# A two-layer mixture-of-experts kernel: plain result rows per token, tiles in three levels of completeness, and a scatter in eight that waits for the one ahead of it

## What is computed

```
x = x + attn_a(layernorm(x))   # grouped causal attention, 8 kv heads x 4, rotary
x = x + ffn(layernorm(x))      # called "f" in the kernel
x = x + attn_b(layernorm(x))   # causal difference attention, 16 heads
x = x + ffn(layernorm(x))      # called "h" in the kernel, same weights

def ffn(x):                    # T = 2048 tokens, 16 experts of width 176
    scores = softmax(x @ Wg.T)                      # (T, 16)
    keep the 2 best of 4 groups of experts, then the 4 best experts (topi)
    combine = 0 everywhere but scores at topi
    h = silu(x @ W1[e]) * (x @ W3[e])               # for each expert e
    y = sum over e of (h @ W2[e]) * combine[:, e]
    z = silu(x @ Ws1.T) * (x @ Ws3.T) @ Ws2.T       # shared expert, width 352
    return y + z
```

## Time and profile before

| | |
|---|---|
| time, median of 3 runs | 1354.8 us (1343.55 to 1356.92) |
| the profiled execution's own time | 1349.85 us |
| its span, first to last instruction | 1348.1 us |
| mean granted TensorE clock | 0.934 of full speed |
| busy: TensorE, VectorE, GpSimd, ScalarE | 1144.7, 873.5, 689.1, 541.6 us |
| DMA | 169.84 MB, mean 126 GB/s |

### The profile page before, as it was taken

How to read it: one execution, slowest core, us unless ns; L and a number is a source line. 1 busy time by engine, 2 the same in 40 slices (tenths; PEclk the granted TensorE clock), 3 DMA queues, 4 the chain that set the end, 5 groups by cost and what they waited for, 6 DMA issues and landing times.

```text
span 1348.1 us, 26055 instructions
## 1 busy us (share of the span) xinstructions
PE 1144.7 (85%) x8706; PEld 614.0 (46%) x8706; DVE 873.5 (65%) x2067; ACT 541.6 (40%) x846; POOL 689.1 (51%) x841
## 2 busy tenths in 40 slices
PE   6888999998899699999288899999779859999990
PEld 2343444342655366566154344444246435665650
DVE  5688899981576145555388899999568523554543
ACT  2124777779431122222032577777844001222210
POOL 4452344544036577767552454545521652787671
PEclk9897999999889799999699899999988978999995
DMA  4424433320825479987754321221062345898868
GB/s 144 144 86 126 122 109 121 106 64 2 287 72 149 150 183 164 158 156 113 192 178 143 108 61 53 62 50 50 3 255 48 113 129 144 168 159 161 153 91 262
DMA packets 145875, 169.84 MB, mean 126 GB/s; under 512 B 20240, under 2 KB 130768, under 8 KB 145232
## 3 DMA queue, kind: packets, MB, share of 16 engines
q1 hardware_dynamic: 115856, 128.79, 32.7%
q0 software_dynamic: 29184, 38.36, 16.7%
q10 hardware_dynamic: 704, 1.02, 0.2%
HBM read 93.29 MB, written 76.18 MB: 126 GB/s over the span
## 4 chain that ended last, share of the span: by engine, by line
PE 57%; DVE 18%; issue 6%; DMA 6%; ACT 6%; POOL 2%; SPq 2%; another core or an unknown queue 1%; POOLq 0%; ACTq 0%; DVEq 0%
PE pair_ps L1996 11%; PE o_ps L1761 9%; ACT arena L849 4%; DVE nm L1123 4%; PE pair_ps L2029 4%; DMA x_slots<-y_sb,slot_i 3%; DVE bm L1123 3%; PE pair_ps L2032 2%; PE t_ps L1787 2%; PE pair_ps L1711 2%; PE pair_ps L1592 2%; PE pair_ps L1691 2%; PE pair_ps L1716 2%; PE pair_ps L2003 2%; PE pair_ps L1686 2%
## 5 line engine op out<-in xcount | busy, mean ns | idle before, releaser
L849 ACT ACTIVATE arena<-pair_ps 128x1024 f32<-128x1024 f32 x320 | 322.9, 1024 | 130.6 <-PE pair_ps L1686 75.9
L625 POOL TENSOR_SCALAR_AFFINE_SELECT arena<-arena 128x512 f32<-128x512 f32 (+1 forms) x320 | 175.0, 547 | 241.4 <-ACT arena L849 240.9
L1123 DVE TENSOR_REDUCE nm<-pair_ps 128x2 f32<-128x1024 f32 (+1 forms) x192 | 232.6, 1222 | 33.4 <-PE pair_ps L1735 29.5
L687 POOL DMA_INDIRECT x_slots<-y_sb,slot_i x128 | 123.6, 966 | 168.0 <-DVE slot_i L1321 94.0
L1761 PE MATMUL o_ps<-arena 128*9 128x512 f32 (+7 forms) x2048 | 176.8, 440 | 4.2 <-POOL arena L625 4.1
L1996 PE MATMUL pair_ps<-arena 128*128 x512 | 168.6, 471 | 2.5 <-ACT arena L900 2.5
L1123 DVE TENSOR_REDUCE bm<-pair_ps 128x8 f32<-128x1024 f32 x128 | 155.3, 1217 | 4.1 <-PE pair_ps L1735 1.0
L703 POOL DMA_INDIRECT y_h<-xnT,dest x80 | 125.3, 1567 | 58.6 <-DVE xnT L1480 31.4
L703 POOL DMA_INDIRECT y_f<-xnT,dest x80 | 124.6, 1558 | 42.0 <-issue 21.2
L1463 DVE TENSOR_TENSOR arena<-arena,pair_ps 128x128 f32<-128x128 f32 x144 | 41.4, 288 | 116.6 <-ACT arena L905 77.1
L1996 PEld LDWEIGHTS pair_ps<-arena 128*128 128x128 f32 x512 | 93.8, 195 | 43.9 <-issue 6.3
(11 more groups left out here) (275 smaller groups left out, 2012.8 us busy)
## 6 DMA issues: line engine op xcount, KB each, us to landing
arena<-x_slots SPq DMA_DIRECT2D x128, 132.5 KB
arena<-in_w SPq DMA_DIRECT2D x4, 2816.0 KB, 18.9
arena<-q_a SPq DMA_DIRECT2D x64, 96.0 KB
arena<-q_b SPq DMA_DIRECT2D x64, 96.0 KB
y_f<-hw SPq DMA_DIRECT2D x11, 512.0 KB, 2.9
y_h<-hw SPq DMA_DIRECT2D x11, 512.0 KB, 2.9
arena<-in_w SPq DMA_DIRECT2D x2, 2048.0 KB, 17.4
arena<-y_f SPq DMA_DIRECT2D x8, 512.0 KB
```

Source lines behind the costliest of these rows:

```text
L625: pool.affine_select(p, p, pattern, ALU.is_ge, 0.0, base=0, channel_multiplier=-1)\
L687: pool.indirect_dma_start(x_slots, bass.IndirectOffsetOnAxis(ap=slot_i[:, t, k:k + 1], axis=0), y_sb[:, t, :], None).then_inc(sm(f"scat{n ...
L849: act.activation(p_ring[:, U % RING, :], pair_ps[:, pair_at("T", n, u)].rearrange("p a c -> p (a c)"), ACT.Exp, scale=SCALE).then_inc(sm(" ...
L1123: dve.tensor_reduce(dst, src, X, ALU.max, negate=not 2 <= u < 4).then_inc(sm("t_max_done"), 1)
```

## The change

**Plain result rows.** The three accumulators are gone. Each layer has one tensor `y_rows[f]` with four rows per token, row 4 x token + k for choice k. A result is written with a plain indirect DMA to these rows, with no addition, one per tile: 72 per layer in place of 80, since a row of a mixed tile has its own destination whatever expert it belongs to. Nothing has to be cleared (22 DMAs go) and x is not stored ahead (`store_x` goes). The slot row grows to EW = 268 floats, since it carries four destinations in place of one token number; `where` is shorter.

**Read-back.** SP reads all four rows of each token, 8 DMAs of 1 MB per layer, in runs of 4 KB. VectorE sums two token tiles at a time (`dve_sum`): 1024 columns, then 512, then 512 into x. `pool_back` goes. The last batch's rows go to a buffer that batch 0 had, so SP waits there until batch 0 has been added. The output is stored in 8 DMAs of 256 KB.

**Three levels.** The tiles' order knows three levels, LEVELS = (8, 10, 12): tiles that are full once token tiles 0 to 7, 0 to 9 or 0 to 11 are placed. SP waits for 32 scatters ahead of tile 0, 40 ahead of tile 16, 48 ahead of tile 24 and 64 ahead of tile 32. `full_tiles` and `places` work on three columns. GpSimd issues 48 scatters ahead of the first result and 16 behind results 0 to 7, two each.

**Mixed tiles** move from 29, 35, ..., 71 to 35, 39, ..., 63.

**Waits.** Each scatter whose number is a multiple of eight (but 0) also waits for the scatter directly ahead of it.

The core of the diff:

```diff
-MIX = tuple(range(29, NJ, 6))
+MIX = tuple(range(35, 64, 4))
...
-EW = E + 2 * TOPK + 1
+EW = E + 3 * TOPK
...
-EARLY_T = 10
-EARLY = 24
-LATE_FIRST = 12
+LEVELS = (8, 10, 12)
+NL = len(LEVELS)
+FIRST_X = 48
...
+        y_rows = {f: nc.dram_tensor(f"y_{f}", (Y_ROWS, E), F32).ap() for f in "fh"}
...
         def sp_attn(sp, s):
-                if s == "a" and n < 22:
-                    f, a = "fh"[n % 2], 0 if n < 2 else 1 if n < 12 else 2
-                    first = ROWS if n < 2 else (n // 2 - 1) % 5 * 4 * P
-                    sp.dma_start(y_acc[f][a][first:first + 4 * P, :]...
...
         def sp_ffn_slots(sp, f):
-            for b in range(B - 1):
-                store_x(b)
             sp.wait_ge(sm("padded"), 16 * NE * (1 + past(f, 1)))
-            for parity in range(2):
-                sp.wait_ge(sm(f"scat{parity}"), 16 * (EARLY_T * TOPK // 2 + past(f, NT * TOPK // 2)))
             for j in range(NJ):
-                if j == 4:
-                    store_x(B - 1)
...
-                if j == EARLY:
-                    for parity in range(2):
-                        sp.wait_ge(sm(f"scat{parity}"), 16 * (NT * TOPK // 2) * (1 + past(f, 1)))
+                for t, first in zip(LEVELS + (NT,), (0,) + tuple(TOPK * t - NE for t in LEVELS)):
+                    if j == first:
+                        for parity in range(2):
+                            sp.wait_ge(sm(f"scat{parity}"), 16 * (t * TOPK // 2 + past(f, NT * TOPK // 2)))
...
         def sp_ffn_back(sp, f):
-            sp.wait_ge(sm("store_second"), 16 * MIXED * (1 + past(f, 1)))
+            rows = y_rows[f][0:ROWS * TOPK, :].rearrange("(t p k) e -> p t k e", p=P, k=TOPK)
             for b in range(B):
-                for a, to in ((0, x_sb), (1, back), (2, back2)):
-                    rows = y_acc[f][a][b * T:(b + 1) * T, :].rearrange("(t p) e -> p t e", p=P)
-                    sp.dma_start(to[:, b * TB:(b + 1) * TB, :], rows).then_inc(sm(f"load{2 * b + a % 2}"), 16)
+                if b == B - 1:
+                    sp.wait_ge(sm(f + "_x"), TB)
+                for u in (0, 2):
+                    sp.dma_start(back[b][:, u:u + 2], rows[:, b * TB + u:b * TB + u + 2])\
+                        .then_inc(sm(f"load{2 * b + u // 2}"), 16)
...
         def pool_ffn(pool, f):
             def scatter(n):
                 if n >= 2:
                     pool.wait_ge(sm(f"scat{n % 2}"), 16 * (n // 2 + past(f, NT * TOPK // 2)))
+                if n > 0 and n % 8 == 0:
+                    pool.wait_ge(sm(f"scat{(n - 1) % 2}"), 16 * ((n + 1) // 2 + past(f, NT * TOPK // 2)))
...
             def result_out(j):
-                if j == 0:
-                    pool.wait_ge(sm("acc_x"), 16 * B * (1 + past(f, 1)))
-                scatter_out(outs.index((j, 0)))
-                if j in MIX:
-                    scatter_out(outs.index((j, 1)))
+                pool.indirect_dma_start(y_rows[f], bass.IndirectOffsetOnAxis(ap=dest[:, j:j + 1], axis=0),
+                                        yt[:, j % XR, :], None).then_inc(sm(f"store{j % XR}"), 16)
...
-            late = range(EARLY_T * TOPK + LATE_FIRST, NT * TOPK)
+            late = range(FIRST_X, NT * TOPK)
...
+        def dve_sum(dve, f, q):
+            b, u, t = q // 2, q % 2 * 2, 2 * q
+            done = q + 1 + past(f, 2 * B)
+            part = back[b][:, u:u + 2]
+            dve.wait_ge(sm(f"load{q}"), 16 * (loads(q) + past(f, loads(q))))
+            dve.tensor_tensor(part[:, :, 0:2, :], part[:, :, 0:2, :], part[:, :, 2:4, :], ALU.add).then_inc(sm("back_half"), 1)
+            dve.wait_ge(sm("back_half"), done)
+            dve.tensor_tensor(part[:, :, 0, :], part[:, :, 0, :], part[:, :, 1, :], ALU.add).then_inc(sm("back_sum"), 1)
+            dve.wait_ge(sm("back_sum"), done)
+            dve.tensor_tensor(x_sb[:, t:t + 2, :], x_sb[:, t:t + 2, :], part[:, :, 0, :], ALU.add).then_inc(sm(f + "_x"), 2)
```

More of the change, by code:

```diff
@@ L327, in loads @@
         def loads(q):
[L330 removed]
+            return row_loads(q, NJ) + 1
         def loaded(f, j):
@@ L1909, in counts @@
                     first = max(t + 1, hf * TH)
-                    n = (TH if hf == 0 else NT + 1) - first + (1 if hf == 1 and t < EARLY_T else 0)
+                    n = (TH if hf == 0 else NT + 1) - first + (sum(t < first_t for first_t in LEVELS) if hf == 1 else 0)
                     mm = pe.matmul(s_ps[:, 0, first * NE:(first + n) * NE].rearrange("p (n e) -> p n e", n=n), ones,
@@ L1917, in scan @@
                 pe.wait_ge(sm("e_full"), 1 + past(f, 1))
-                pe.matmul(s_ps[:, 1, 0:1], upper, full[:], start=True, stop=True, skip_group_check=True)\
+                pe.matmul(s_ps[:, 1, 0:NL], upper, full[:], start=True, stop=False, skip_group_check=True)
+                pe.matmul(s_ps[:, 1, NL:2 * NL], ones, full[:], start=False, stop=True, skip_group_check=True)\
                     .then_inc(sm("e_scan"), 1)
```

185 lines of the change are left out of this document (71 added, 114 removed).

## The result

| | before | changed |
|---|---|---|
| median (range), us | 1354.26 (1343.55 to 1358.14, 6 runs) | 1365.66 (1363.63 to 1367.17, 6 runs) |
| profiled execution, us | 1349.85, span 1348.1 | 1367.17, span 1365.2 |
| granted TensorE clock | 0.934 | 0.925 |

The ratio is 1.0107, 95% interval 1.0071 to 1.0142: the changed kernel is 1% slower, where 1328 us and a range up to 1352 us had been forecast.

A forecast was written before the change was run, and what follows sets the result against it. TensorE was taken to bound the expert loop, VectorE the attention. From the profiled 1349.85 us, -8.7 (f -7.9 -4.5 +5.5, h +0.8 -4.5 +1.9) and -15 for the stall gave 1326, plus 2.5 toward the median: 1328 us, range 1308 to 1352.

The forecast's parts named there:

- The start of f: Layer f's expert loop starts sooner after the shared expert, its first load wanting 32 scatters, not 40: -8.7, -7.9 with arithmetic.
- The ends of the loops: From VectorE's last result to SP's first read, GpSimd is less behind with plain issues: -4.5 us in each layer.
- The stall in h: Layer h's shared-expert stage, 25.1 us longer than f's: drains shorten instruction waits, -15 us, bounds 0 and -25.1.
- engines without instructions while scatters are always in flight: Reading of h's shared-expert stall, from 34 us without instruction packets beside a busy software queue; called not shown.
- GpSimd is not the bound, so nothing: Expert loops: 72 plain results at 0.96 us replace 80 accumulating ones at 1.61; no time gained or lost.
- Taken as 0, bound +5 us a layer: Early expert loop: result buffers and evictions might wait behind late scatters and drains; 0 us, at most +5 a layer.
- rival D: The same stall also comes up in layer f's shared stage, 25 us, with h's unchanged: 1369 us; chance 0.08.
- The ring: Rival C: result ring or sums cost their upper bounds, +5 to +10, while the stall shrinks: 1338 us; chance 0.13.
- The slack of 2.6 us: Early expert loop: result 7 lands near 498, result 15 wants its buffer near 501, leaving 2.6 us.
- The read-back of f: Behind layer f, VectorE's four-row sums add 9.6 us, 4 of them hidden: +5.5 us, bounds +1 and +10.
- The mixed tiles': Expert loops: mixed tiles move from 29...71 to 35...63, still eight, so TensorE's work is the same.
- The median: Profile lies 4.95 us under the median; half, 2.5 us, added to 1326, as that may be more of the stall.

The follow-up runs named there:

- calm groups: Groups of runs whose traces have 0 to 2 slow SP register instructions each; kernel before at 1329.0, 1333.6 and 1329.3 us.
- adding version: Changed kernel with results written by adding DMAs into cleared rows, in place of plain ones: 1346.8 us, ratio 0.9892 to the kernel before.
- groups 2 to 4: Three sets of side-by-side runs: spread late scatters, repeats, fewer waits or GpSimd sums on the changed kernel; kernel before at 1329.0, 1333.6, 1329.3 us.
- group 3: Repeat runs side by side: kernel before unchanged 1331.7 us, changed 1330.2, changed with one late scatter a result 1317.2, changed without added waits 1313.5.
- two held-up groups: Groups 1 and 5, with SP's slow-instruction raster; kernel before 1372.4 and 1370.6 us, changed kernel without added waits 1416.9 and 1413.9.

## Why the prediction was wrong, point by point

**The start of f** was right: forecast -8.7 and 0.8 back for arithmetic, so -7.9, measured 12.5 to 3.6 us, -8.9. In h +0.8 was forecast, and the gap went from 3.8 to 3.3. In calm groups, where h has no stall to hide it, this part is worth more than forecast: 11.4 to 3.8 and 12.6 to 3.4 us, 16.8 in all.

**The ends of the loops** were right: -3.9 and -4.0 against -4.5 each. The adding version shows that 3.2 of them are the plain DMA.

**The stall in h**: the size was near (forecast -15, measured 93.2 to 70.6, -22.6), and the drains are its cause, shown by the kernel before with the waits alone (70.2 us) and by the changed one without them (107.9). The reading "engines without instructions while scatters are always in flight" is not borne out. Scatters or results are in flight in every trace that has the stall, but the same density holds nothing up in groups 2 to 4. And the sign that the reading rested on, no instruction packet in 34 us, is no sign of a stall. The kernel before has none in layer f from 400 to 439 us either (DMA view), and TensorE is busy all 39 us there (windows view):

```profile
q0 software_dynamic: 1155, 3.27, 23.9%
q1 hardware_dynamic: 1568, 2.14, 22.6%
...
400.00:439.00 39.00, 39.00 (x123) 22.03 (x122) 21.27 (x81) 4.17 (x7) 23.00 (x24) 1.00 0.46 139
```

Whether instructions come late or are carried out slowly is open; SP's come one by one on the raster. The rule of the Trainium skill, page "DMA: Bandwidth & Descriptors", section "Queues, rings and completion order", that a DMA engine takes turns between queues, agrees with the calm groups, where SP's queue takes 36.9% of the engines beside the software queue's 26.9%; nothing here explains the other groups by it.

**"GpSimd is not the bound, so nothing" and "Taken as 0, bound +5 us a layer"** is the step that failed. It was worth +21.3 and +24.1 us. The prediction saw a stall that came with dense scatters, saw that the change makes results plain and so GpSimd's issues in the loop denser (from 1.61 to 0.96 us each), and did not put the two together: rival D was priced only for the shared expert, at 0.08. In the measured pair the holding up is the whole of it. There, up to result 16, no result of VectorE waits for a store. What ends its waits in f (one line's instructions, us and times) is, in the changed kernel of the prediction's measurement and then of group 3:

```profile
  remote: 8.7, 2
  PE pair_ps L1993: 4.4, 7
...
  DMA y_f<-xnT,dest: 10.9, 4
  PE pair_ps L1993: 4.4, 7
```

The ring shows only in calm groups, as a second and smaller error of the same step. In group 3 it costs 5.9 us in f (55.0 against 49.1 without the waits) and 9.7 in h, so the bound of +5 was too small even with the engines free. The slack of 2.6 us was worked out with waits of 1.3 us; they cost 1.7 to 2.3 (five of them 11.5 us in f, 8.4 in h), and result 0 left later. In group 3 the same kernel's stretch is 17.8 us shorter in f (72.8 to 55.0) and 16.6 in h than in the measured pair, so that much at least goes with the kind of group.

**The read-back of f** was sized within its bounds: +5.5 forecast, bounds +1 and +10, measured +9.7 in this pair and +5.5 in group 3 (374.6 to 380.1). The first scores of attention b come 4.1 us later after SP's read (44.6, 40.5 before), where 5 was forecast, and 3.1 in group 3. Another 5.2 us of the 9.7 come in the next 50 us, where the last of VectorE's sums stand, so in this pair fewer of them are hidden than the 4 us taken. The durations were right: the profile of the changed kernel, one line's instructions, gives 1.22 and 0.69 us.

```profile
L1204 DVE TENSOR_TENSOR arena<-arena x12: 1190/1219/1226, 670.0 to 1359.9; 128x1024 f32<-128x1024 f32 x12
...
L1206 DVE TENSOR_TENSOR arena<-arena x12: 691/692/692, 671.2 to 1361.1; 128x512 f32<-128x512 f32 x12
```

In h it was +2.2 against +1.9.

**The mixed tiles'** new positions were put at nothing. The stretch behind result 32 is 1.5 us longer (eight of them there, seven before) and that ahead of it 1.1 shorter, which fits them; no run tested it alone.

**The median.** The prediction took the stall for systematic, since even the fastest of three runs, 1343.55 us, was only 6 us under the profile. It goes with the group instead: the kernel before ran at 1329 to 1334 us in three of five groups. Where nothing is held up, the changed kernel's profile is 6.3 us shorter (1335.3 to 1329.0), near the forecast of -8.7 without the stall. That nearness is luck: the gap in h gave 9.3 us where +0.8 was forecast, and the stretches to result 16 took 10.0 where nothing was.

## What to carry to other kernels

Where a trace has a long wait whose releaser is "issue" or "remote" and other engines stop with it, find what the one engine that keeps working is doing, and then ask of every edit whether it makes that engine's work denser, wherever it stands; an edit that makes an issue cheaper can cost more than it gives. A backlog on an engine that is "not the bound" is spent from the ring between it and the bound: work out the slack of each buffer with the waits at their measured price, and spread deferred work at the pace of the consumer (one scatter a result, not two). Before a result of 1% is explained, run the kernel before again at another time: here its own median moved by 3%.

## What was not expected of the hardware

In two groups and in the prediction's measurement, while GpSimd issued long rows of indirect DMAs 1.27 to 1.5 us apart, SP's plain register instructions came on a raster of 0.70 to 0.72 us and ScalarE, TensorE and VectorE stood for 12 to 21 us at a time; GpSimd itself kept its pace. In three other groups nothing of the kind came up, not even beside 43 issues in a row. One wait for a landing in eight scatters (1.7 to 2.3 us each) kept the shared-expert stages at 68 to 71 us in each group, against 97 to 108 without it in the two held-up groups. A DMA view without instruction packets for 39 us goes with engines that are all at work, so it says nothing of a stall. A plain indirect DMA of 128 rows of 1 KB occupies GpSimd for 0.96 us, as the scatter does, and an adding one for 1.6; with adding ones the end of a loop, from VectorE's last result to SP's read, is 3.2 us longer.
